# DeltaNet mixer with a top-2 MoE on one core: written-out steps, two load queues, and the FFN's residual sum moved from VectorE to TensorE and ScalarE

## The chip, the cores and the metric

One core of a Trainium2 chip runs the whole program. The metric is the device time of one execution in microseconds, median of several runs. TensorE is PE in the profile (PEld its weight loads), VectorE is DVE, ScalarE is ACT, GpSimd is POOL, SyncE is SP; SPq is the queue on which SyncE issues transfers.

## The reference

The input `x` is 8 x 192 x 16 x 16 in fp32: 8 sequences of 256 tokens with 192 channels. A mixer and an FFN follow each other, both with a residual sum.

```python
# mixer: t = layernorm over channels of x, heads of 16, 12 heads
q = l2norm(silu(t @ Wq)); k = l2norm(silu(t @ Wk)); v = silu(t @ Wv)
beta = sigmoid(t @ Wb)
# for every token, per head:
#   u_t = beta_t * (v_t - S_{t-1}^T k_t);  S_t = S_{t-1} + k_t u_t^T;  o_t = S_t^T q_t
x = x + (t + o @ Wo)
# FFN: h = layernorm(x), 8 experts of width 192, the top 2 weighted, a shared one of width 768
probs = softmax(h @ router_w); gates, idx = top_k(probs, 2), normalised
routed = sum_e dense_g[e] * ((silu(h @ w_gate[e]) * (h @ w_up[e])) @ w_down[e])
shared = (silu(h @ ws_gate) * (h @ ws_up)) @ ws_down
alpha = sigmoid(h @ sg_w + sg_b)
out = x + alpha * shared + (1 - alpha) * routed
```

## The kernel before

The 256 tokens are cut into 16 chunks of 16 tokens (`NC = 16`, `T = 16`); with 8 sequences a chunk has 128 tokens, one for each partition. A pipeline runs over steps c = -3 to 18. In step c, DVE runs the scan of chunk c, token by token. Around it the engines do the preparation of chunks c+1 to c+3 (functions `A_...`: norm, transposes, projections, silu, l2 norms), the mixer's output and the router of chunk c-1 (`Fa_...`, `G_...`), the FFN of chunks c-1 and c-2 (`Fb_...`, `unit`, `hidden`) and the result of chunk c-3 (`Fc_...`).

The scan on DVE has 16 iterations a step, and each iteration four operations, each done for two halves of the heads: `Pr` (L1150, product with the state), `u` (L1152, sum), `bank` (L1154, the key times u), `SH` (L1158, the new state). After each of these groups is a numbered slot, 64 a step, at which other DVE work is inserted by `at(slot, distance, function)`. The keys come from PE: `fill` (L358) multiplies `KR`, the keys of the chunk, with a selector, eight times a step for two iterations each; it waits until the state of an earlier pair is done. `KR` and `QB` (the queries, spread over partitions) are written to a scratch in DRAM and read back by SyncE's queue (`scratch_k`, `load_k`, `scratch_q`, `spread_q`). POOL multiplies states with queries (`reading`, `PQ` L778) and sums them up (`summing`, L785, L802). Its `rsqrt` (L767) makes the factors of both norms in one operation, for which DVE's `A_bias` waits.

The order of every engine's work in a step is a list written out by hand; semaphores alone couple the engines. Steps -3 to 3 and 12 to 18 are written out, steps 4 to 11 are a hardware loop of four turns with two steps each (`chunks`, L161 to L169). At the end of a step DVE waits for its chained operations and clears their semaphore `s_chain`; ACT and POOL clear theirs at the start of the next.

The FFN's hidden width is 12 units of 192 (`UN = 12`): 8 experts and 4 quarters of the shared one. Each unit is five fp32r matmuls of 384 columns (`Fb_up`, L397 to L401), because both operands are split into a high and a low part. ACT makes `sg` and `ug` from them (`unit`, L610, L611), POOL multiplies them (`hidden`, L823), PE transposes the product (`Fb_turn`, L409), ACT copies it (`hidden`, L621), and PE multiplies by `Wd` in fp32 (`Fb_down`, L421) in five groups into the bank `bDn`. DVE's `Fc_res` (L960) then adds the mixer's output `xh` to the bank, PE transposes `res` and ACT copies it into `xT`, which is stored.

The split of the up weights is made once, at the start. The first 128 rows come into `raw0`; ACT rounds them to `Whi0` (`weights_hi0`, L592) and POOL makes the rest (`weights_lo0`, L808). The last 64 rows come twice into the halves of `raw1`; ACT (`weights_hi1`, L601) and POOL (`weights_1`, L813) split them. All loads are issued by SyncE: in `load` before the first step `x` of four chunks, the projection weights, small weights and `raw0`; in `load_later` in step -1 the rest of `x`, `raw1` and `Wd`. In POOL's list of step 0, `weights_1(0)` and `weights_1(1)` stand ahead of `rsqrt(0)`.

Of the kernel before, what the change touches and what calls it, by code (L numbers as in the profile page):

```python
# [13 lines left out]
NC = L // T  # L14
P = 128
# [16 lines left out]
def build(nc, x, Wq, Wk, Wv, Wb, Wo, router_w, w_gate, w_up, w_down, ws_gate, ws_up, ws_down, sg_w, sg_b, out):  # L32
    ctx = ExitStack()
    with ctx:
# [128 lines left out]
        def chunks(eng, step):  # L163

            for c in range(-3, 4):
                step(c, c % 2)
            with eng.Fori(0, 4) as k:
                for j in range(2):
                    step(eng.snap(k * 2 + (4 + j)), j)  # L169
            for c in range(12, NC + 3):  # L170
                step(c, c % 2)

        def stage(c, par, d, fn, *args):

            n = c + d
            if not isinstance(n, int) or 0 <= n < NC:
                fn(n, (par + d) % 2, *args)

        def once(c, at, fn, *args):

            if isinstance(c, int) and c == at:
                fn(*args)

        def later(n, by):

            return not isinstance(n, int) or n >= by
# [9 lines left out]
        def scratch(slot, lo, n):  # L196

            return bKB[slot // 8 % 2][:, 2 * BR * G + lo:2 * BR * G + lo + n]

        @block.sync  # L200
        def _(sp):
# [41 lines left out]
            def load_up(i, to, lo, hi):  # L243

                for half, we, ws in ((0, w_gate, ws_gate), (H, w_up, ws_up)):
                    sp.dma_start(to[:, 0:E, half:half + H], we[:, lo:hi, :].rearrange("e c h -> c e h")).then_inc(s_wu[i], 16)  # L246
                    sp.dma_start(to[:, E:UN, half:half + H], ws[lo:hi, :].rearrange("c (s h) -> c s h", h=H)).then_inc(s_wu[i], 16)  # L247

# [5 lines left out]
            def load():  # L254
# [26 lines left out]
            def step(c, par):  # L281
# [5 lines left out]
                if isinstance(c, int) and c == -1:  # L287
                    load_later()
                if isinstance(c, int) and c == EARLY + 3:
                    sp.wait_ge(s_outc, EARLY)  # L290
                    store(0, EARLY * T)

            load()
            chunks(sp, step)
# [5 lines left out]
        def _(pe):  # L300
# [34 lines left out]
            def A_qk(a, p):  # L335
                if isinstance(a, int) and a == 0:
# [8 lines left out]
            def A_vb(a, p):  # L345
                if isinstance(a, int) and a == 0:
# [14 lines left out]
            def Fa_o(f, p):  # L361
                pe.wait_ge(s_otok, f + 1)
                pe.wait_ge(s_qks, f + 4 if not isinstance(f, int) else min(f + 4, NC))
                turn(bFa, otok).then_inc(s_ocp, 1)

            def Fa_y(f, p):
                if isinstance(f, int) and f == 0:
# [12 lines left out]
            def Fa_logits(f, p):  # L380
                if isinstance(f, int) and f == 0:
# [5 lines left out]
            def Fb_up(f, p, n):  # L387

                if isinstance(f, int) and f == 0 and n == 0:
# [23 lines left out]
            def Fb_down(f, p, g):  # L413
                lo, hi = GRP[g]
                if isinstance(f, int) and f == 0 and g == 0:
# [12 lines left out]
            def step(c, par):  # L428
                at = partial(stage, c, par)
                at(-2, Fb_up, 3)  # L430
                at(-3, Fb_down, 3)
                at(0, fill, 2)
                at(-2, Fb_up, 4)
                at(2, A_vb)
                at(2, A_qk)
                at(0, fill, 3)
                at(-2, Fb_up, 5)
                at(-1, Fa_o)
                at(-3, Fb_down, 4)
                at(0, fill, 4)  # L440
                at(3, A_x)
                at(-1, Fa_y)
                at(-2, Fb_turn, 0)
                at(-2, Fb_up, 6)
                at(-2, Fb_up, 7)
                at(-2, Fb_turn, 1)
                at(-2, Fb_up, 8)
                at(0, fill, 5)
                at(-3, Fc_out)
                at(-1, Fa_h)  # L450
                at(-2, Fb_up, 9)
                at(-2, Fb_up, 10)
                at(0, fill, 6)
                at(-1, Fa_logits)
                at(-2, Fb_turn, 2)
                at(-2, Fb_down, 0)
                at(0, fill, 7)
                at(-2, Fb_up, 11)
                at(-1, Fb_up, 0)
                at(-2, Fb_down, 1)  # L460
                at(1, fill, 0)
                at(-2, Fb_turn, 3)
                at(-2, Fb_down, 2)
                at(-1, Fb_up, 1)
# [3 lines left out]
                at(-2, Fb_turn, 4)  # L468

            pe.wait_ge(s_id, 2)  # L470
            pe.wait_ge(s_sel, T // 2)
            chunks(pe, step)

        @block.scalar
        def _(act):
# [9 lines left out]
            def A_xs(a, p):  # L485
                if later(a, 1):
                    act.wait_ge(s_xT, a)
                if isinstance(a, int) and a == FIRST:
# [90 lines left out]
            def Fa_exp(q, p):  # L579
# [3 lines left out]
                if isinstance(q, int) and q == 0:  # L583
# [38 lines left out]

            def Fc_out(q, p):
# [11 lines left out]
            def step(c, par):  # L635
                def table(n, name):

                    if (not isinstance(n, int) or 0 <= n < NC) and tables[0] != name:
# [3 lines left out]
                if n[0]:  # L642
                    act.sem_clear(s_act)
                    n[0] = 0
                at = partial(stage, c, par)
                at(-3, unit, 10)
                table(c - 2, LN_EXP)
                at(-2, Fa_exp)
                at(0, place, 0)
                table(c + 1, LN_EXP)  # L650
                at(1, A_inv)
                table(0, SILU)
                at(-3, hidden, 2)
                at(-3, unit, 11)
                once(c, 1, weights_hi1, 4)
                at(-2, unit, 0)
                at(2, A_h)
                at(2, A_xh)
                at(1, A_khi)
                once(c, 0, weights_hi0, 7)  # L660
                at(-3, hidden, 3)
                at(-2, unit, 1)
                once(c, 1, weights_hi1, 5)
# [543 lines left out]
```

## Time and profile before

| | us |
|---|---|
| median of 3 runs | 538.85 (537.14 to 539.02) |
| the profiled execution | 535.79 |
| its span, first to last instruction | 534.1 |
| mean granted TensorE clock | 0.938 of full |

The profile is of one execution. A timeline row gives start, length, engine, line, operation, written tile and read tiles, and in brackets how long the engine was idle before it and what released it. Rows with "x2" merge two operations of one kind. Matmuls overlap in time, so the distance of their starts says more than their lengths. "issue" in the chain is time in which the engine waited for nothing that the profile shows.

### The profile page before, as it was taken

The numbers are of one execution on the slowest core, as the hardware profiler recorded it, in microseconds if no ns is written. First come the engines' busy times: TensorE is split into PE (matmuls) and PEld (weight loads), VectorE is DVE, ScalarE is ACT, GpSimd is POOL, SyncE is SP. The second block draws the span as 40 slices with busy tenths as digits, with TensorE's granted clock in tenths as the row PEclk, the third lists the DMA queues.
The fourth block names the chain that finished last, engine by engine and source line by source line (L and its number), as shares of the span: only waits on it lengthen the run. The fifth ranks groups of instructions, "written<-read, shape, count | busy, mean of one in ns | idle before, by whom it ended". The sixth has DMA issues, their size and how long they took to land.

```text
span 534.1 us, 11599 instructions
## 1 busy us (share of the span) xinstructions
PE 439.0 (82%) x2464; PEld 384.2 (72%) x2464; DVE 435.6 (82%) x2546; ACT 330.8 (62%) x927; POOL 410.9 (77%) x525
## 2 busy tenths in 40 slices
PE   1552025799999999799979999899999998989996
PEld 0431013579888888688877978698988897979996
DVE  4177078999999999899979997999999999999300
ACT  2680053658585858485847767485858584746853
POOL 4471099989898989789895989698989899987341
PEclk9996555589999999999999999999999999999999
DMA  3659933232323222222222232313232323210300
GB/s 86 192 128 184 189 110 106 75 79 78 91 67 83 74 84 75 75 77 73 74 68 52 64 86 68 84 59 95 61 89 68 83 76 86 72 60 2 104 2 16
DMA packets 44682, 44.01 MB, mean 82 GB/s; under 512 B 19857, under 2 KB 36433, under 8 KB 44625
## 3 DMA queue, kind: packets, MB, share of 16 engines
q1 hardware_dynamic: 44624, 43.44, 31.2%
q14 instruction: 45, 0.36, 0.2%
q8 instruction: 13, 0.21, 0.2%
HBM read 37.13 MB, written 6.29 MB: 81 GB/s over the span
## 4 chain that ended last, share of the span: by engine, by line
DVE 65%; PE 10%; issue 6%; POOL 6%; SPq 6%; DMA 3%; ACT 1%; DVEq 1%; POOLq 0%; ACTq 0%
DVE Pr L1150 14%; DVE bank L1154 14%; DVE u L1152 14%; DVE SH L1158 12%; PE bank L421 3%; POOL PQ L778 3%; DMA W_unsplit<-in_L_ffn_ws_up_dram 2%; POOL PQ L785 2%; DVE st L907 2%; SPq L247 1%; DVE ss L991 1%; SPq L241 1%; PE bank L409 1%; SPq L246 1%; DVE mv L908 1%
## 5 line engine op out<-in xcount | busy, mean ns | idle before, releaser
L823 POOL TENSOR_TENSOR hid<-sg,ug 128x192 f32<-128x192 f32 x192 | 109.8, 598 | 39.4 <-ACT ug L611 36.9
L1150 DVE TENSOR_TENSOR Pr<-SH,bank 128x96 f32<-128x96 f32 x512 | 106.1, 251 | 17.8 <-ACT Pr L555 10.6
L778 POOL TENSOR_TENSOR PQ<-SH,QB 128x768 f32<-128x768 f32 x62 | 112.6, 1838 | 0.9 <-DVE SH L1158 0.9
L1154 DVE TENSOR_TENSOR bank<-bank,u 128x96 f32<-128x96 f32 x512 | 108.9, 261 | 0.0
L785 POOL TENSOR_TENSOR PQ<-PQ 128x768 f32<-128x768 f32 (+2 forms) x93 | 103.2, 1109 | 6.0
L1152 DVE TENSOR_REDUCE u<-Pr 128x6 f32<-128x102 f32 x512 | 107.7, 254 | 0.0
L421 PE MATMUL bank<-Wd,hidT 128*128 128x192 f32 x576 | 106.6, 326 | 0.0
L1158 DVE TENSOR_TENSOR SH<-SH,bank 128x96 f32<-128x96 f32 x512 | 106.2, 252 | 0.0
L421 PEld LDWEIGHTS bank<-Wd,hidT 128*128 128x128 f32 x576 | 93.7, 190 | 0.0
L610 ACT ACTIVATE sg<-bank 128x192 f32<-128x192 f32 x192 | 63.1, 329 | 44.1 <-PE bank L401 31.0
L358 PE MATMUL bank<-KR,Sel 128*128 128x384 f32 x128 | 55.1, 435 | 39.3 <-DMA KR<-k_scratch 25.6
L397 PE MATMUL bank<-Whi,hiT 128*128 128x384 f32 x192 | 73.9, 385 | 1.8 <-issue 1.8
L401 PE MATMUL bank<-W,loT 128*128 128x384 f32 x192 | 65.6, 342 | 0.0
L399 PE MATMUL bank<-Whi,loT 128*128 128x384 f32 x192 | 65.6, 341 | 0.0
L398 PE MATMUL bank<-Wlo,hiT 128*128 128x384 f32 x192 | 65.6, 341 | 0.0
L400 PE MATMUL bank<-W,hiT 128*128 128x384 f32 x192 | 65.4, 341 | 0.0
L358 PEld LDWEIGHTS bank<-KR,Sel 128*128 128x128 f32 x128 | 26.0, 205 | 44.5 <-DMA KR<-k_scratch 26.1
L611 ACT ACTIVATE ug<-bank,gate 128x192 f32<-128x192 f32 x128 | 53.4, 417 | 0.0
L621 ACT ACTIVATE hidT<-bank 128x512 f32<-128x512 f32 (+1 forms) x80 | 44.4, 555 | 14.3 <-PE bank L409 13.0
L639 ACT ACT_TABLE_LOAD x38 | 48.8, 1283 | 0.7
L409 PE MATMUL bank<-ident,hid 128*128 128x128 f32 x288 | 46.8, 280 | 0.4 <-POOL hid L823 0.2
L397 PEld LDWEIGHTS bank<-Whi,hiT 128*128 128x128 f32 x192 | 36.8, 192 | 5.0 <-issue 4.7
(146 smaller groups left out, 816.3 us busy)
## 6 DMA issues: line engine op xcount, KB each, us to landing
QB<-q_scratch SPq DMA_DIRECT2D x64, 384.0 KB
k_scratch<-khl SPq DMA_DIRECT2D x64, 48.0 KB, 2.6
KR<-k_scratch SPq DMA_DIRECT2D x32, 96.0 KB, 2.4
q_scratch<-qn SPq DMA_DIRECT2D x64, 24.0 KB, 1.6
Wd<-in_L_ffn_w_down_dram SPq DMA_DIRECT2D x1, 1152.0 KB, 12.7
out_dram<-xT SPq DMA_DIRECT2D x1, 896.0 KB, 4.1
Wlo_unsplit<-in_L_ffn_w_gate_dram SPq DMA_DIRECT2D x1, 768.0 KB, 5.4
Wlo_unsplit<-in_L_ffn_w_up_dram SPq DMA_DIRECT2D x1, 768.0 KB, 7.9
```

The lines of the kernel that those rows point to most:

```text
L358: mm(bKB[f % 2][:, 0:2 * BR * G], Sel[:, f].rearrange("p b x e -> p (b x e)"), KR[:, p, :], start=True, stop=True).then_inc(s_fill, 1)
L397: mm(to, hiT[:, p, 0:P], Whi0[:, n], start=True, stop=False)
L398: mm(to, hiT[:, p, 0:P], Wlo0[:, n], start=False, stop=False)
L399: mm(to, loT[:, p, 0:P], Whi0[:, n], start=False, stop=False)
L421: last = mm(bDn[:, 0:C], hidT[:, turn_half(g), k - lo, :], Wd[:, k, :], start=(k == 0), stop=(k == KT - 1))
L778: tt(PQ[:, at * BR * HP:(at + n) * BR * HP].rearrange("p (i b h) d -> p i b (h d)", i=n, b=BR), SH[:, lo:lo + n].rearrange("p i b h d -> p ...
L785: chained(tt(PQ[:, :, 0:w], PQ[:, :, 0:w], PQ[:, :, w:2 * w], ALU.add))
L823: tt(hid[:, r * H:(r + 1) * H], sg[:, m % RING], ug[:, m % RING], ALU.mult).then_inc(s_hid, 1)
L1150: v = each(lambda br: count(tt(Pr[:, br, i, :, 0:D], prev[:, br], KB[:, br], ALU.mult)), Sb)
L1152: v = each(lambda br: count(nc.vector.tensor_reduce(u[:, i % 2, br], Pr[:, br, i], X, ALU.add, negate=True)), v)
L1154: v = each(lambda br: count(tt(KB[:, br], KB[:, br], u[:, i % 2, br].unsqueeze(2).to_broadcast([P, HP, D]), ALU.mult)), v)
L1158: ins = tt(SH[:, i, br], prev[:, br], KB[:, br], ALU.add)
```

## The change

The hardware loop goes: all 22 steps are written out. The three clears of the chain semaphores go, and DVE's last wait of a step with them; the first iteration of a step waits for the state operations of the step before, half by half.

The first part of the up weights (`raw0`) is issued by ACT in step -3, after its first `A_xs`. The second part (`raw1`) moves into SyncE's `load`, before the first step. `load_later` keeps `x` and `Wd`.

DVE's `Fc_res` goes. PE puts one more product at the head of the down sum, identity times `xh`, into the same bank, and ACT copies the bank into `res`.

The lists of PE, ACT, POOL and DVE's slots are drawn anew. The step's border lies elsewhere in the lists: `Fb_up 3` and `4`, `fill 2`, `Fb_down 3`, `A_vb` and `A_qk` stand at the end of PE's list for the chunk that used to be handled at the start of the next step, and the same holds for ACT and POOL.

```diff
-        def chunks(eng, step):
-
-            for c in range(-3, 4):
+        def chunks(step):
+
+            for c in range(-3, NC + 3):
                 step(c, c % 2)
-            with eng.Fori(0, 4) as k:
-                for j in range(2):
-                    step(eng.snap(k * 2 + (4 + j)), j)
-            for c in range(12, NC + 3):
-                step(c, c % 2)
...
-                load_up(0, raw0, 0, C0)
+                load_up(sp, 1, raw1[0:C1], C0, C)
+                load_up(sp, 1, raw1[C1:P], C0, C)
 
             def load_later():
 
                 load_x(1, FIRST * T, L)
-                load_up(1, raw1[0:C1], C0, C)
-                load_up(1, raw1[C1:P], C0, C)
...
+                if g == 0:
+                    mm(bDn[:, 0:C], ident[:, :], xh[:, bass.ds(f, 1), :].rearrange("p z c -> p (z c)"), start=True, stop=False)
                 for k in range(lo, hi):
-                    last = mm(bDn[:, 0:C], hidT[:, turn_half(g), k - lo, :], Wd[:, k, :], start=(k == 0), stop=(k == KT - 1))
+                    last = mm(bDn[:, 0:C], hidT[:, turn_half(g), k - lo, :], Wd[:, k, :], start=False, stop=(k == KT - 1))
...
+            def Fc_res(q, p):
+                act.wait_ge(s_dg, q * NG + NG)
+                if later(q, 1):
+                    act.wait_ge(s_outp, q)
+                f(res[:, :], bDn[:, 0:C], ACT.Copy).then_inc(s_res, 1)
...
-            def Fc_res(q, p):
-                dve.wait_ge(s_dg, q * NG + NG)
-                if later(q, 1):
-                    dve.wait_ge(s_outp, q)
-                tt(res[:, :], bDn[:, 0:C], xh[:, bass.ds(q, 1), :].rearrange("p z c -> p (z c)"), ALU.add).then_inc(s_res, 1)
...
-                if n[0]:
-                    dve.wait_ge(s_chain, n[0])
-                if running:
-                    dve.wait_ge(s_pair, c * 8 + 8)
-                if n[0]:
-                    dve.sem_clear(s_chain)
-                n[0] = 0
```

The new lists, from the step's start (a stroke stands for the chunk after; only what the prediction speaks of is named in full):

```
PE    fill3 up5 down4 Fa_o A_x up6 Fa_y fill4 turn0 up7 up8 turn1 fill5 up9 Fc_out Fa_h fill6
      up10 up11 logits down0 turn2 fill7 down1 up0' turn3 fill0' up1' down2 fill1' up2' A_h
      turn4 up3' fill2' down3 up4' A_vb A_qk
ACT   A_xs (step -3: load raw0) place1 unit3 unit4 silu_v silu_qk Fa_oc sq unit5 unit6 hidden0
      unit7 Fc_res place0' Fa_h unit8 unit9 Fa_hT Fc_out unit10 hidden1 unit11 Fa_exp hidden2
      A_inv unit0' A_h A_xh A_khi hidden3 unit1' hidden4 A_hT unit2'
POOL  hidden6 rsqrt reading0 hidden7-10 summing0 hidden11 A_kn A_qn A_vn hidden0' reading1
      summing1 hidden1'-3' A_klo hidden4' hidden5'
DVE   slot 14 A_low, 19 A_z, 23 Fa_otok, 27 A_vT, 30 A_stats, 31 Fa_add A_var Fa_stats Fa_var,
      35 Fa_bias, 46 Fa_split, 47 A_ss A_bias, 48 to 58 router as before
```

Before, the same entries of PE read cyclically from `fill3`: `fill3 up5 Fa_o down4 fill4 A_x Fa_y turn0 up6 up7 turn1 up8 fill5 Fc_out Fa_h up9 up10 fill6 logits turn2 down0 fill7 up11 up0' down1 fill0' turn3 down2 up1' fill1' up2' A_h turn4 up3' down3 fill2' up4' A_vb A_qk`, and DVE had `A_z` at 20, `A_stats` at 31, `Fa_add Fa_stats A_var Fa_var` at 32, `Fa_bias Fc_res A_ss` at 36, `Fa_split` at 44, `A_vT` at 47, `A_bias` at 48. The splits of the up weights move too: `weights_1(0)` to `(3)` now stand at the end of POOL's list of step -1, behind `rsqrt(-1)`, and `weights_1(4)` to `(7)` in step 0 behind `rsqrt(0)`.

## Rows read from the trace of the kernel before

**Rows 1.** Page, parts 1 and 2: engines' busy time; clock and DMA by slices of 13.35 us.
```profile
PE 439.0 (82%) x2464; PEld 384.2 (72%) x2464; DVE 435.6 (82%) x2546; ACT 330.8 (62%) x927; POOL 410.9 (77%) x525
...
PEclk9996555589999999999999999999999999999999
...
DMA  3659933232323222222222232313232323210300
```

**Rows 2.** Page, part 4: the chain that ended last, by engine.
```profile
DVE 65%; PE 10%; issue 6%; POOL 6%; SPq 6%; DMA 3%; ACT 1%; DVEq 1%; POOLq 0%; ACTq 0%
```

**Rows 3.** Stretches, one step outside the loop: PE, PEld, DVE, ACT, POOL, clock, DMA.
```profile
131.50:158.30 26.80, 25.96 (x156) 23.21 (x155) 26.28 (x158) 19.18 (x57) 24.17 (x31) 1.00 0.30 79
```

**Rows 4.** Chain in order of time (start, us): first scan operations, a pause, last matmuls.
```profile
104.75 0.42 DVE Pr L1150 x2
...
131.31 0.42 DVE Pr L1150 x2
...
158.52 0.42 DVE Pr L1150 x2
...
212.77 2.80 issue
...
385.06 0.42 DVE Pr L1150 x2
...
411.88 0.42 DVE Pr L1150 x2
...
527.56 1.97 PE bank L421 x12
```

**Rows 5.** Chain in order of time, 210 to 217 us: what surrounds that pause.
```profile
212.71 0.06 DVEq L167
```

**Rows 6.** DVE timeline: start, length, line, operation, tiles, [idle before].
```profile
146.09 0.35 DVE L960 TENSOR_TENSOR res<-bank,xh 128x192 f32<-128x192 f32 x1
...
146.36 0.55 DVE L991 TENSOR_REDUCE ss<-sq 128x24 f32<-128x384 f32 x1
...
463.31 0.42 DVE L1150 TENSOR_TENSOR Pr<-SH,bank 128x96 f32<-128x96 f32 x2 [0.30 <-DVE SH L1158]
```

**Rows 7.** PE timeline, same step: a wait, and starts around a change of type.
```profile
140.21 0.33 PE L310 MATMUL bank<-ident,otok 128*128 128x128 f32 x1 [0.55 <-DVE otok L1021]
...
147.55 0.44 PE L397 MATMUL bank<-Whi,hiT 128*128 128x384 f32 x1
...
147.83 0.34 PE L398 MATMUL bank<-Wlo,hiT 128*128 128x384 f32 x1
...
148.01 0.34 PE L399 MATMUL bank<-Whi,loT 128*128 128x384 f32 x1
```

**Rows 8.** Timelines of SyncE's queue, DVE, ACT and PE, 0 to 80 us, in order of time.
```profile
15.13 2.45 SPq L247 DMA_DIRECT2D Wlo_unsplit<-in_L_ffn_ws_up_dram  x1
...
30.55 0.42 DVE L1150 TENSOR_TENSOR Pr<-SH,bank 128x96 f32<-128x96 f32 x2 [0.23 <-ACT Pr L555]
...
40.06 2.22 SPq L246 DMA_DIRECT2D W_unsplit<-in_L_ffn_w_gate_dram  x1
...
55.12 0.92 SPq L278 DMA_DIRECT2D Wd<-in_L_ffn_w_down_dram  x1
...
63.21 4.03 SPq L206 DMA_DIRECT2D k_scratch<-khl  x4
...
65.61 1.35 ACT L601 ACTIVATE hid<-W_unsplit 64x384 fp32r<-64x384 f32 x3 [24.06 <-DMA W_unsplit<-in_L_ffn_ws_up_dram]
...
68.85 0.15 DVE L925 TENSOR_SCALAR rstd<-rs 128x1 f32<-128x1 f32 x1 [18.44 <-POOL rs L767]
...
74.99 1.01 PE L358 MATMUL bank<-KR,Sel 128*128 128x384 f32 x2 [24.43 <-DMA KR<-k_scratch]
...
75.71 0.42 DVE L1150 TENSOR_TENSOR Pr<-SH,bank 128x96 f32<-128x96 f32 x2 [1.43 <-PE bank L358]
```

**Rows 9.** A stretch of 2 us in the start: columns as in rows 3.
```profile
18.00:20.00 2.00, 0.00 (x0) 0.00 (x0) 0.73 (x3) 1.92 (x5) 0.67 (x1) 1.00 1.08 332
```

More of the change, by code:

```diff
@@ L468, in step @@
                 at(-2, Fb_turn, 4)
+                at(-1, Fb_up, 3)
+                at(1, fill, 2)
+                at(-2, Fb_down, 3)
+                at(-1, Fb_up, 4)
+                at(3, A_vb)
+                at(3, A_qk)
             pe.wait_ge(s_id, 2)
             pe.wait_ge(s_sel, T // 2)
-            chunks(pe, step)
+            chunks(step)
         @block.scalar
@@ L648, in step @@
[L648 to L662, printed above, removed]
@@ L692, in step @@
                 once(c, 1, weights_hi1, 8)
+                once(c, 1, weights_hi1, 9)
+                at(1, place, 0)
                 at(-1, Fa_h)
-                at(-2, hidden, 1)
+                once(c, 1, weights_hi1, 10)
+                once(c, 1, weights_hi1, 11)
                 at(-2, unit, 8)
-                once(c, 0, weights_hi1, 1)
-                once(c, 1, weights_hi1, 9)
-                once(c, -1, weights_hi0, 6)
-                once(c, 0, weights_hi1, 2)
-                once(c, 1, weights_hi1, 10)
@@ L701, in step @@
-                once(c, 0, weights_hi1, 3)
+                at(-2, unit, 9)
                 at(-1, Fa_hT)
                 at(-3, Fc_out)
-                once(c, 1, weights_hi1, 11)
-                at(-2, unit, 9)
+                at(-2, unit, 10)
+                at(-2, hidden, 1)
+                at(-2, unit, 11)
+                once(c, -1, weights_hi0, 5)
+                table(c - 1, LN_EXP)
+                at(-1, Fa_exp)
+                at(-2, hidden, 2)
+                table(c + 2, LN_EXP)
@@ new lines, in step @@
+                at(2, A_inv)
+                table(0, SILU)
+                once(c, -1, weights_hi0, 6)
+                once(c, -1, weights_hi0, 7)
+                at(-1, unit, 0)
+                at(3, A_h)
+                once(c, 0, weights_hi1, 5)
+                at(3, A_xh)
+                at(2, A_khi)
+                once(c, -1, weights_hi0, 8)
+                at(-2, hidden, 3)
+                at(-1, unit, 1)
+                once(c, -1, weights_hi0, 9)
+                at(-2, hidden, 4)
@@ L773, in products @@
                     pool.wait_ge(s_QB[half], c * 32 + 32)
-                    if half or not isinstance(c, int) or c > 0:
+                    if half or c > 0:
                         pool.wait_ge(s_oT, c * 2 + half)
@@ L787, in reading @@
             def reading(c, p, half):
-                if half == 0 or not isinstance(c, int) or c < NC - 1:
+                if half == 0 or c < NC - 1:
                     products(c, half, 0)
@@ L792, in summing @@
             def summing(c, p, half):
-                if half == 1 and isinstance(c, int) and c == NC - 1:
+                if half == 1 and c == NC - 1:
                     return
```

240 lines of the change are left out of this document (114 added, 126 removed).

## Prediction, on record before the changed kernel ran

> **What bounds the kernel now.** I read five views, in this order: the page's totals, its chain, the chain in order of time, the timelines of single engines over one step, and the timelines of the first 80 us.
>
> The totals show no engine idle for long: PE and DVE are both busy for 82% of the span, POOL for 77% [rows 1]. The chain settles which of them counts: 65% of it is DVE, 10% PE, and 6% "issue", time in which nothing that the profile shows is awaited [rows 2]. So the kernel is three pieces: a start-up, the sixteen scan steps paced by DVE, and a tail after the scan.
>
> The scan can be measured by the starts of each step's first `Pr` operation. Step 2 starts at 104.75, step 3 at 131.31, step 4 at 158.52, step 12 at 385.06, step 13 at 411.88 [rows 4] and step 15 at 463.31 [rows 6]. Steps 4 to 11 are those of the hardware loop. Step 12, written out, takes 411.88 - 385.06 = 26.82 us; the eight loop steps take 226.54, or 28.32 each. The extra time has a visible part: a pause of 2.80 us on DVE at the back edge [rows 4], between two instructions of L167, the loop's own line [rows 5]. There are three such pauses in the chain.
>
> Within a written-out step DVE works almost without a gap (26.28 of 26.80 us). PE is busy for 25.96 of the same 26.80 [rows 3], so it is a near second: only 0.84 us of room, of which 0.55 is a wait for `otok` [rows 7]. POOL (24.17) and ACT (19.18) have more.
>
> The start-up holds one large stall. Step 0 starts at 30.55. Some thirteen of its sixteen iterations later DVE stops for 18.44 us, waiting for POOL's `rs`; POOL's list has `weights_1` ahead of it, which waits for ACT's `hid` L601, and that stood for 24.06 until the second half of the up weights had landed at 65.6. SyncE's queue was meanwhile still issuing loads (the second half's from 40.06 to 55.12, then `Wd`), and came to the keys of step 1 only at 63.21; PE's first matmul of step 1 ran at 74.99 and step 1 started at 75.71 [rows 8].
>
> **Part by part: steps written out.** The loop's eight steps at the length of step 12 take 8 x 26.82 = 214.56, so 11.98 less than now: 3 x 2.80 = 8.4 are the pauses, 3.6 the slower steps between them. Step 3, which ends with the entry to the loop, took 27.21 against 26.82: 0.4 more. Together -12.4 us. The instructions that run are the same ones, and a written-out step has no pause of that kind in the rows I read. (The Trainium skill, page Advanced Engine Details and Errata, section Control Flow Timing, gives a compare-and-branch about 108 ns. By it the three back edges would give 0.3 us back and the sum would be 8 us higher; the measured pause is 2.80 us each, and the row decides. The Trainium skill's page Runtime: NRT & Kernel Launch, section Instruction fetch mechanics, has a reason that no row here shows: a taken branch out of the fetched window must fetch its target.)
>
> **No clears.** Each step ends with DVE waiting for all its chained operations, then a semaphore clear. DVE stands idle for 0.30 us before the next step's first `Pr` [rows 6]. The wait for the state itself stays, but DVE can issue under it. I take the 0.30; over the 14 ends of steps 2 to 15, -4.2 us (bounds: nothing, if the state's own latency is the wait, and 4.2). The clears of ACT and POOL lie beside idle time and are costed at nothing.
>
> **The residual sum.** `Fc_res` leaves DVE: it starts at 146.09 and the next operation at 146.36 [rows 6], so 0.27 us. In steps 3 to 15, 13 x 0.27 = -3.5 us. It becomes one fp32 product of 192 columns on PE, which issues as two matmuls, ahead of the down groups. Twelve such take 1.97 us [rows 4], so two are 0.33 us. ACT gets a copy of about 0.33, hidden in its 7.6 us of room per step; if that cover were gone, 13 x 0.33 = 4.3 us. The copy waits for the last down group of the item before, and behind it stand `place(1, 0)`, `Fa_h` and `Fa_hT` in ACT's order; that group ran early in the step, so I expect no wait there. PE's `Fc_out` now stands behind `Up 9`, which covers the copy.
>
> **Orders redrawn.** Read cyclically, PE's, ACT's and POOL's lists are nearly the old ones: their start is turned by a few entries, and the operations keep their place against DVE's slots. What differs: `Fb_down 4` now stands ahead of `Fa_o`, so that it fills most of the 0.55 wait for `otok` [rows 7]; `logits` come one `Up` later and `Fa_split` two slots later; `A_vT` moves from slot 47 to 27, where its input was ready in the step before; `Fa_add`'s latency now hides `A_var` (at most 0.1 us a step, taken as nothing). Against it, PE changes from fp32 to fp32r 11 times a step instead of 9, and a first fp32r matmul after fp32 delays the next start to 0.28 instead of 0.18 [rows 7]: up to 0.2 us.
>
> This sets a new bound. DVE's step becomes 26.82 - 0.30 - 0.27 = 26.25. PE's need becomes 25.96 + 0.33 = 26.29 with no wait at all, and 27.13, if its 0.84 of waits stays as it is. The bounds of PE's excess over DVE are thus 0 (overlapping ends overstate its busy time) and 0.88 a step, 11.4 us over 13 steps. Since the largest wait is filled, I take the lower part: 0.1 a step, +1.3 us.
>
> **Up weights over two queues.** The first half (`raw0`, 2.3 MB by its shape) is issued by ACT, right after the first `xs`; the second half (another 2.3 MB, written twice into half the partitions) follows the small weights on SyncE at once, not after step 0's queries. What SyncE still has to load after these is `x` (1.15 MB) and `Wd` (1.7 MB).
>
> The cost: of the four issues of `raw0` the last alone held SyncE for 2.45 us [rows 8]. On ACT they stand ahead of `A_h(0)`, which all of chunk 0 follows; the projection weights, which DVE's split awaits, share the engines with `raw0`. And chunk 0's keys now queue behind the second half. I take 2.5 us of delay for step 0 (bounds 0, and 9: about 2 from the issues and 7 for 2.3 MB at the 332 GB/s of rows 9).
>
> The gain: the eight issues of the second half held SyncE's queue from 40.06 to 55.12 [rows 8], since it was full; the DMA engines were at 0.9 in these slices [rows 1]. With them gone from there, step 1's keys come 15.1 us earlier. Step 1 so starts at 75.71 - 15.1 + 2.5 = 63.1, an advance of 12.6. DVE would be there sooner: step 0 needs 19.9 us to its stall (68.85 - 18.44 - 30.55) and 5.4 from there to its end (75.71 - 1.43 - 68.85), 25.3 in all, so 30.55 + 2.5 + 25.3 = 58.4. The keys are what is late next. Step 1 took 104.75 - 75.71 = 29.04 with pauses that POOL's remaining weight work caused; step 2 took 26.56. I count 2.5 back. Start-up: -15.1 us (bounds -8.6 with all 9 of delay, -22.3 if step 1 waits for DVE alone and nothing is delayed).
>
> (A rule that speaks against this part is in the Trainium skill, page DMA: Bandwidth & Descriptors, section Issuing engines are not separate DMA queues: all issuers share the same 16 engines and a second one saves only issue time. By it two queues in themselves would give nothing and the sum would lose the whole 15.1 us; the stretch at 18 us shows the engines full, share 1.08, with one queue [rows 9], so the trace agrees. My gain rests on the order of the loads, not on their rate.)
>
> **Tail.** After the scan PE is full, and two residual products lie in it: +0.65 us.
>
> **Sum.** Span 534.1 - 12.4 - 4.2 - 3.5 + 1.3 - 15.1 + 0.65 = 500.9. The profiled execution took 535.79, 1.7 above its span: 502.6. The median of the runs, 538.85, lies 3 us above that execution, and their lowest, 537.14, 1.4 above; I forecast 503.5.
>
> **The rivals.**
> - TensorE becomes the pace: its 0.84 of waits stay beside the new product, 27.13 a step instead of 26.35, 13 x 0.78 = +10: 513.5. For it: 25.96 busy of 26.80. Against it: the largest wait is filled by the new order.
> - The loads hold the start anyway: the same bytes pass, now in front of step 0, and the 15.1 are not gained: 518.6. For it: engines at share 1.08 [rows 9]. Against it: over the first three slices they stood at 0.3, 0.6 and 0.5 [rows 1], so there is free time before 40 us for these bytes.
> - The start is hidden wholly: step 1 waits for DVE alone, and nothing is delayed, 7.2 us better: 496.3. Against it: 4.4 MB (`x`, `Wd` and the queries' 1.5) still pass ahead of step 1's keys.
> - Slower than before: PE's clock. It was granted at 0.5 (1.2 GHz) in the slices from 53 to 107 us [rows 1], while PE mostly waited for the scan's states and for keys. If it stays at 1.2 GHz in steps with full FFN work, PE's 26.3 us become up to 52.6, +26 a step. Two such steps more than now cancel the 35 us gained and give 503.5 + 52 = 555.5; it decides from 1.4 steps. For it: step 2 is now reached sooner. Against it: in the slice after PE had taken up its full work the clock was 0.8, by step 3 1.00 [rows 1, 3], and nothing in that changes.
>
> **How the numbers follow.** Forecast 0.62, TensorE 0.20, loads hold 0.07, start hidden 0.08, clock 0.02, and 0.01 that several small losses leave no change. Likeliest 503.5. The range reaches below the hidden start by 2 us of its bounds (494) and past the TensorE case (516); what it leaves out above is 0.10. About 0.5% (2.7 us) is what a measurement can tell from no change; faster 0.97, same 0.01, slower 0.02.
>
> **What would show it.** No pause of 2.8 us on DVE; steps 26.2 to 26.4 apart, with DVE's idle time before `Pr` at step ends gone. If TensorE is the pace, DVE's waits for `bank` L358 grow. In the start: ACT's `Whi` before 20 us, no 24 us wait of ACT or POOL, step 0 at 33, step 1 at 63.1 behind PE's wait for `KR`. Wrong would be: steps above 27, or step 1 after 70.

## The result and the profile after

The changed kernel takes 508.38 us (median of 4 runs, 507.11 to 509.27), the kernel before beside it 538.61 (4 runs): a ratio of 0.944, 95% interval 0.941 to 0.947. The forecast was 503.5 with a range of 494 to 516. The profiled execution took 509.27, with a span of 507.4; the prediction's sum for the span was 500.9, so 6.5 us are to be accounted for.

First the page of the changed kernel: busy times, granted clock and DMA share in slices of 12.7 us, and the chain by engine (they answer to [rows 1, 2]).

```profile
PE 438.0 (86%) x2496; PEld 391.9 (77%) x2496; DVE 431.1 (85%) x2530; ACT 330.8 (65%) x943; POOL 412.3 (81%) x525
...
PEclk9999999999999999999999999999999999999999
...
DMA  7939733232324232322323232323232323300300
...
DVE 64%; PE 14%; SPq 7%; POOL 6%; issue 3%; DMA 3%; ACT 1%; DVEq 0%; POOLq 0%; ACTq 0%
```

PE's and DVE's shares are up to 86% and 85%, in a span 26.7 us shorter. "issue" fell from 6% to 3% of the chain. In this execution PE's clock doesn't fall in the start: it is at 9 or more (the level of 2.4 GHz) in every slice. The DMA's load has moved to the front: slices 1, 2, 4 and 5 stand at 7, 9, 9 and 7.

One step, as [rows 3] (columns: length, then busy time of PE, PEld, DVE, ACT and POOL, clock, DMA share, GB/s):

```profile
120.90:147.30 26.40, 26.03 (x158) 23.87 (x157) 26.20 (x159) 19.29 (x58) 24.19 (x31) 1.00 0.29 80
```

Then the starts of steps 0, 1, 2, 3, 4 and 15, in DVE's timeline (start, length, engine, line, operation, tiles, in brackets the idle time before):

```profile
34.50 0.41 DVE L1143 TENSOR_TENSOR Pr<-SH,bank 128x96 f32<-128x96 f32 x2
...
67.37 0.42 DVE L1143 TENSOR_TENSOR Pr<-SH,bank 128x96 f32<-128x96 f32 x2 [7.41 <-PE bank L352]
...
94.56 0.42 DVE L1143 TENSOR_TENSOR Pr<-SH,bank 128x96 f32<-128x96 f32 x2
...
120.92 0.42 DVE L1143 TENSOR_TENSOR Pr<-SH,bank 128x96 f32<-128x96 f32 x2
...
147.27 0.42 DVE L1143 TENSOR_TENSOR Pr<-SH,bank 128x96 f32<-128x96 f32 x2
...
436.13 0.42 DVE L1143 TENSOR_TENSOR Pr<-SH,bank 128x96 f32<-128x96 f32 x2
```

No pause of 2.8 us [rows 4, 5] is left, nor the idle 0.30 ahead of `Pr` [rows 6]. A normal step takes 147.27 - 120.92 = 26.35 us, where 26.2 to 26.4 was forecast. From step 2 to step 15 it is 436.13 - 94.56 = 341.57 for thirteen steps, where the prediction had 340.3. From step 15's start to the end it is 71.3, forecast 70.87 (its own end without the 0.30 and without `Fc_res`, plus the residual products). So 1.3 + 0.4 of the 6.5 us arise after the start-up, and 4.9 in it: step 2 starts at 94.56, forecast 89.65. Step 1 starts at 67.37, forecast 63.1.

The start-up in timelines of ACT's queue, DVE, SyncE's queue and PE (beside [rows 8]):

```profile
6.96 2.30 ACTq L199 DMA_DIRECT2D Wlo_unsplit<-in_L_ffn_ws_up_dram  x1
...
15.04 0.47 DVE L965 CAST Wphi<-Wp 128x588 fp32r<-128x588 f32 x1 [6.30 <-DMA Wp<-in_L_conv_Wb_dram]
...
39.02 8.37 SPq L272 DMA_DIRECT2D Wd<-in_L_ffn_w_down_dram  x1
...
47.42 7.71 SPq L273 DMA_DIRECT2D Wd<-in_L_ffn_ws_down_dram  x1
...
55.18 3.69 SPq L207 DMA_DIRECT2D k_scratch<-khl  x4
...
66.65 1.01 PE L352 MATMUL bank<-KR,Sel 128*128 128x384 f32 x2 [12.08 <-DMA KR<-k_scratch]
```

ACT's last issue of `raw0` stood 2.30 us. One sign of the prediction failed here: ACT's `Whi`, expected before 20 us, is first written at 26.82. DVE's split of the projection weights came 4.5 us later than it does where `raw0` isn't loaded beside them (10.58, in experiment 6), and step 0 began at 34.50 instead of 30.55: 3.95 of delay, estimated 2.5. In the queue of SyncE the eight issues that had taken 15.1 us are gone, as said. But the two issues of `Wd`, which had taken 63.21 - 55.12 = 8.1 us [rows 8], now take 16.1, and the keys of step 1 begin at 55.18: only 8.0 earlier. (The second issue of `x`, just ahead of `Wd`'s, shrank from 5.38 us to 0.65.) PE waits 12.08 us for `KR`.

The same stretch as shares of time and rates, columns as above:

```profile
10.00:12.00 2.00, 1.31 (x4) 0.53 (x4) 0.00 (x0) 0.60 (x3) 0.00 (x0) 1.00 1.10 319
...
22.00:24.00 2.00, 0.00 (x0) 0.00 (x0) 1.09 (x5) 1.94 (x5) 0.69 (x1) 1.00 1.11 215
...
28.00:30.00 2.00, 0.98 (x5) 0.97 (x5) 0.42 (x1) 1.83 (x5) 1.97 (x3) 1.00 0.35 77
```

The 16 engines are full while the up weights pass (from 8 to about 27 us), and free at 28. The rate falls from 319 to 215 GB/s at the same share, when only `raw1`, whose transfers write 64 partitions each, is left.

### The profile page after: what moved, and what is told of

The parts are those of the page before. It is cut to its first block, busy times and chain, and to the rows that moved or that the text cites. A ratio compares the mean times of both kernels' runs of the same rounds, so it can differ in the third digit from the quotient of the medians.

```text
span 507.4 us, 10651 instructions
## 1 busy us (share of the span) xinstructions
PE 438.0 (86%) x2496; PEld 391.9 (77%) x2496; DVE 431.1 (85%) x2530; ACT 330.8 (65%) x943; POOL 412.3 (81%) x525
## 4 chain that ended last, share of the span: by engine, by line
DVE 64%; PE 14%; SPq 7%; POOL 6%; issue 3%; DMA 3%; ACT 1%; DVEq 0%; POOLq 0%; ACTq 0%
DVE Pr L1143 14%; DVE bank L1147 14%; DVE u L1145 13%; DVE SH L1151 11%; PE bank L417 5%; POOL PQ L779 2%; POOL PQ L786 2%; SPq L272 2%; DVE st L905 2%; SPq L273 2%; PE bank L403 1%; DMA k_scratch<-khl 1%; DMA Wp<-in_L_conv_Wb_dram 1%; PE bank L391 1%; PE bank L393 1%
## 5 line engine op out<-in xcount | busy, mean ns | idle before, releaser
L824 POOL TENSOR_TENSOR hid<-sg,ug 128x192 f32<-128x192 f32 x192 | 112.6, 602 | 39.6 <-ACT ug L607 19.1
L417 PEld LDWEIGHTS bank<-Wd,hidT 128*128 128x128 f32 x576 | 96.2, 190 | 0.0
L352 PE MATMUL bank<-KR,Sel 128*128 128x384 f32 x128 | 56.4, 445 | 22.5 <-DMA KR<-k_scratch 13.3
L403 PE MATMUL bank<-ident,hid 128*128 128x128 f32 x288 | 45.1, 275 | 0.0
L403 PEld LDWEIGHTS bank<-ident,hid 128*128 128x128 f32 x288 | 35.5, 141 | 4.0 <-issue 1.9
```

Of the source, the lines that this page charges most:

```text
L352: mm(bKB[f % 2][:, 0:2 * BR * G], Sel[:, f].rearrange("p b x e -> p (b x e)"), KR[:, p, :], start=True, stop=True).then_inc(s_fill, 1)
L403: last = tr(bHt[:, (k - lo) * P:(k - lo + 1) * P], hid[:, k % (KT // 2) * P:(k % (KT // 2) + 1) * P], ident[:, :])
L824: tt(hid[:, r * H:(r + 1) * H], sg[:, m % RING], ug[:, m % RING], ALU.mult).then_inc(s_hid, 1)
```

## The experiments

Ratios are to the kernel before on the same chip, with 95% intervals; each normal step is read between the starts of `Pr`. Spans are of the one traced execution, and among the four executions of one kernel they differ by up to 3.6 us (experiment 3). A difference of a few us is therefore read from where it arises in the trace: step 0, for one, starts at 34.3 to 34.8 in all seven traces with the changed kernel's order of loads ahead of it.

**1. Written out only.** The kernel before with its loop replaced, nothing else.

```diff
-            for c in range(-3, 4):
-                step(c, c % 2)
-            with eng.Fori(0, 4) as k:
...
+            for c in range(-3, NC + 3):
+                step(c, c % 2)
```

> The kernel before with the hardware loop written out and nothing else. Theory (the loop cost 12.4 us: three pauses of 2.8 and slower steps between them): steps 4 to 11 at 26.8 us each, span 521.7, ratio 0.977. Rival (the slower loop steps are not the loop's doing but the length of a full step): only the 8.4 us of the pauses go, steps 4 to 11 stay at 27.2, span 525.7, ratio 0.984. Rival (written-out code has to be fetched and stalls in its turn): no gain, ratio 1.00.

Measured: 524.59 us, ratio 0.974 (0.969 to 0.978), span 521.9. Two neighbouring steps in what used to be the loop, in DVE's timeline:

```profile
238.72 0.42 DVE L1145 TENSOR_TENSOR Pr<-SH,bank 128x96 f32<-128x96 f32 x2 [0.30 <-DVE SH L1153]
...
265.54 0.42 DVE L1145 TENSOR_TENSOR Pr<-SH,bank 128x96 f32<-128x96 f32 x2 [0.30 <-DVE SH L1153]
```

265.54 - 238.72 = 26.82, the length of step 12 before, and steps 4 to 12 take 26.81 to 26.85. The span fell by 12.2 us, forecast 12.4. The pause and the slow steps both belonged to the loop.

**2. No clears.** Experiment 1, and no clears or waits for them at a step's end; the first iteration waits for the state itself.

```diff
-                if n[0]:
-                    dve.wait_ge(s_chain, n[0])
-                if running:
-                    dve.wait_ge(s_pair, c * 8 + 8)
-                if n[0]:
-                    dve.sem_clear(s_chain)
-                n[0] = 0
```

> As the run with the loop written out, and without the waits and clears at the ends of steps. Theory: 0.3 to 0.4 us less a step, so steps at 26.5, span 4.2 to 5.6 us below that of the run with the loop written out. Rival (the next step's first product waits for the state anyway): no difference between the two.

Measured: 520.63 us, ratio 0.966 (0.962 to 0.970), span 518.6.

```profile
291.19 0.42 DVE L1141 TENSOR_TENSOR Pr<-SH,bank 128x96 f32<-128x96 f32 x2
...
317.68 0.42 DVE L1141 TENSOR_TENSOR Pr<-SH,bank 128x96 f32<-128x96 f32 x2
```

317.68 - 291.19 = 26.49, so 0.33 less a step, a little more than the 0.30 of idle time. From step 2 to step 15 that makes 4.0 us, since two of the thirteen steps took 26.67 and 26.84. Step 2 began at 105.47, 0.8 later than in experiment 1, for a reason that isn't known, so the span fell by 3.3 only, less than the 4.2 to 5.6 expected. The rival (no difference) is out.

**3. The loads only.** Experiment 1 with the new order of loads, all other orders old.

```diff
+                once(c, -3, load_up, act, 0, raw0, 0, C0)
...
-                load_up(0, raw0, 0, C0)
+                load_up(sp, 1, raw1[0:C1], C0, C)
+                load_up(sp, 1, raw1[C1:P], C0, C)
```

> The loop written out, and the up weights loaded as in the changed kernel (first half by ACT, second half ahead of step 0), with the old orders of work. Theory (the order of the loads makes the start-up gain): step 1 starts at about 67 as in the changed kernel instead of 75.7, span 8 to 11 us below the run with the loop written out. Rival (the gain needs the new places of the weight splits in POOL's and ACT's lists too): step 1 later than 70, or step 1 itself 29 us long as before instead of 27.2.

Measured: 512.79 us, ratio 0.950 (0.946 to 0.955), span 512.9. Starts of steps 0, 1 and 2:

```profile
34.77 0.42 DVE L1145 TENSOR_TENSOR Pr<-SH,bank 128x96 f32<-128x96 f32 x2 [0.22 <-PE bank L352]
...
67.78 0.42 DVE L1145 TENSOR_TENSOR Pr<-SH,bank 128x96 f32<-128x96 f32 x2 [7.80 <-PE bank L352]
...
94.60 0.42 DVE L1145 TENSOR_TENSOR Pr<-SH,bank 128x96 f32<-128x96 f32 x2 [0.30 <-DVE SH L1153]
```

Step 1 begins within 0.4 us of where the changed kernel has it, step 2 at the same time, 10.1 earlier than in experiment 1 (104.68). The order of loads alone makes the whole gain of the start-up. Of the 10.1, 1.1 are lost behind step 2, most of it in the last step, where DVE waits once for PE (0.82), so the span fell by 9.0. By the medians it is 11.8: the traced execution was the slowest of four here (spans 509.3 to 512.9) and the fastest of four in experiment 1.

**4. The sum back on DVE.** The changed kernel with `Fc_res` on DVE at slot 35, without PE's product and ACT's copy.

```diff
-                if g == 0:
-                    mm(bDn[:, 0:C], ident[:, :], xh[...], start=True, stop=False)
...
-                at(-3, Fc_res)
...
+                    at(35, -3, Fc_res)
```

> The changed kernel with the residual sum back on DVE (at slot 35) and neither the extra product nor ACT's copy. Theory (DVE paces the steps, PE's product lies in its idle time): steps of 26.36 become 26.63, span 3.5 us longer, the tail 0.65 shorter, ratio to the changed kernel 1.006. Rival (PE is as much the pace, so the move gave nothing): steps stay at 26.36 and the span is the same or shorter.

Measured: 509.6 us, ratio 0.944 (0.940 to 0.949), span 508.9.

```profile
307.53 0.42 DVE L1141 TENSOR_TENSOR Pr<-SH,bank 128x96 f32<-128x96 f32 x2
...
334.15 0.42 DVE L1141 TENSOR_TENSOR Pr<-SH,bank 128x96 f32<-128x96 f32 x2
```

334.15 - 307.53 = 26.62: the move is worth 0.26 us a step, estimated 0.27. The span differs from the changed kernel's by 1.5 only. From step 2 to step 15 the kernel takes 2.5 us more; 0.9 comes back at the end (step 15 and the tail take 70.4 here, 71.3 with the products on PE). The rest of 13 x 0.26 lies in step 2, which takes 26.36 in both kernels, and in one long step less (below). The expected 3.5 less 0.65 was missed by about half. The medians, 508.38 and 509.6, were taken on different chips, and the ratios to the kernel before are both 0.944. So the move's worth is shown in the steps; a net gain in time is not shown.

**5. `Wd` later.** The changed kernel, with the two issues of `Wd` behind SyncE's work of step 0, that is behind step 1's keys and queries.

```diff
                 if c == -1:
                     load_later()
+                if c == 0:
+                    load_down()
```

> The changed kernel with the load of Wd moved behind step 1's keys and queries. Theory (step 1 waits for its keys, which queue behind Wd on the same queue): PE's wait of 12.1 us for the keys and DVE's of 7.4 go, step 1 starts at about 60 instead of 67.4, span 7 us shorter, about 500. Rival (the keys are late for another reason, or Wd then delays step 2's): less than 3 us.

Measured: 501.87 us, ratio 0.932 (0.929 to 0.935), span 500.0. DVE's, PE's and SyncE's timelines:

```profile
34.38 0.41 DVE L1148 TENSOR_TENSOR Pr<-SH,bank 128x96 f32<-128x96 f32 x2
...
59.29 1.22 PE L357 MATMUL bank<-KR,Sel 128*128 128x384 f32 x2 [4.86 <-DMA KR<-k_scratch]
...
60.02 0.42 DVE L1148 TENSOR_TENSOR Pr<-SH,bank 128x96 f32<-128x96 f32 x2 [0.19 <-PE bank L357]
...
66.48 0.46 SPq L275 DMA_DIRECT2D Wd<-in_L_ffn_w_down_dram  x1
```

Step 1 starts at 60.02, and DVE was idle only 0.19 before it, though PE still waited 4.86 for `KR`: the keys now come just as DVE ends step 0. The span is 7.4 shorter, all of it at step 1 (67.37 - 60.02 = 7.35). `Wd` itself, issued at 66.48 with only the queries just ahead of it, takes 0.46 and 0.77 us of the queue instead of 8.37 and 7.71. The long issues have moved once more: the four of step 1's keys, now next behind the queries and `x`, take 8.4 us (42.43 to 50.87) instead of 3.69.

**6. `raw0` later.** The changed kernel, with ACT's four issues behind `A_hT(0)`.

```diff
-                once(c, -3, load_up, act, 0, raw0, 0, C0)
                 at(3, A_hT)
+                once(c, -3, load_up, act, 0, raw0, 0, C0)
```

> The changed kernel with ACT's four loads issued only after its copy of chunk 0's transposed input, about 11.9 us, instead of at 5.1. Theory (the first half of the up weights slows the projection weights on the shared DMA engines, by 4.4 us): the projection weights land near 10.7 as before the change, step 0 starts at 30.5 to 31.5 instead of 34.5; but step 1 waits for its keys behind Wd, so the span falls by less than 4, 0 to 4 us. Rival (the weights then come too late for the splits or for chunk 0's keys): step 0 not earlier, span the same or longer.

Measured: 511.24 us, ratio 0.949 (0.946 to 0.953), span 509.8.

```profile
10.58 0.47 DVE L965 CAST Wphi<-Wp 128x588 fp32r<-128x588 f32 x1 [2.06 <-DMA Wp<-in_L_conv_Wb_dram]
...
38.34 0.42 DVE L1143 TENSOR_TENSOR Pr<-SH,bank 128x96 f32<-128x96 f32 x2 [4.80 <-PE bank L352]
```

The projection weights are there at 10.58 again, but step 0 starts at 38.34, 3.8 later than in the changed kernel: the same bytes now keep the engines full until about 33 us, and the scratch round of chunk 0's keys stands in them. The expected start of step 0 (30.5 to 31.5) was missed, and the rival's account holds: what was saved ahead of the projection is paid at the keys.

**7. One queue.** The changed kernel, with both halves issued by SyncE, `raw0` first.

```diff
-                once(c, -3, load_up, act, 0, raw0, 0, C0)
...
+                load_up(sp, 0, raw0, 0, C0)
                 load_up(sp, 1, raw1[0:C1], C0, C)
```

> The changed kernel with both halves of the up weights issued by SyncE, first half first, none by ACT. Theory (one queue is served in order): the projection weights land near 10.7, but chunk 0's keys wait behind 4.6 MB, so step 0 starts at 35 to 38 and the span is 0 to 3 us longer than the changed kernel's. Rival (the second queue is what made the gain): step 0 after 40, span more than 5 us longer. Rival (the second queue was of no use): step 0 before 34.5, span shorter.

Measured: 513.41 us, ratio 0.953 (0.950 to 0.958), span 512.3, so 4.9 more than the changed kernel's. PE's first product of step 0's keys:

```profile
39.01 1.01 PE L353 MATMUL bank<-KR,Sel 128*128 128x384 f32 x2 [10.24 <-DMA KR<-k_scratch]
```

PE waits 10.24 us for chunk 0's keys, and step 0 starts at 39.73 instead of 34.50. The result lies between the first expectation and its rival. What it shows is that the second queue is worth about 5 us here, because its bytes start sooner: SyncE has 21 smaller issues ahead of `raw0` and comes to it at 13.30, ACT at 5.12. From 8 to 16 us the engines' share is 0.19, 0.33, 0.08 and 0.55 with one queue and 1.08 to 1.14 with two; the full stretch ends at about 34 us instead of 27.

**8. The product three times.** The changed kernel with the residual product made thrice (two surplus ones, 4 more issues on PE, 0.65 us a step).

```diff
-                    mm(bDn[:, 0:C], ident[:, :], xh[...], start=True, stop=False)
+                    for last in (True, True, False):
+                        mm(bDn[:, 0:C], ident[:, :], xh[...], start=True, stop=last)
```

> The changed kernel with the residual product made three times into the same bank (the first two are overwritten), 0.65 us more of PE work in each step. Theory (DVE is the pace and PE has about 0.4 us of room a step): steps grow by 0.25 us at most, from 26.36 to 26.6, the tail by 1.3; span 2 to 5 us longer. Rival (PE has no room left): 0.65 a step and in the tail, 10 us longer. Rival (PE has ample room): only the tail, 1.3 us.

Measured: 511.96 us, ratio 0.952 (0.949 to 0.955), span 509.3.

```profile
279.07 0.42 DVE L1144 TENSOR_TENSOR Pr<-SH,bank 128x96 f32<-128x96 f32 x2
...
305.49 0.42 DVE L1144 TENSOR_TENSOR Pr<-SH,bank 128x96 f32<-128x96 f32 x2
```

305.49 - 279.07 = 26.42: 0.65 us more of PE's work lengthens a step by 0.06. PE's room shows in its waits for DVE's `loT` (columns: us in all, times, longest), first in this kernel, 94 to 420 us:

```profile
PE bank L299 <- DVE loT L953: 0.5, 1, 0.5
```

and in the changed kernel, over the same stretch:

```profile
PE bank L299 <- DVE loT L952: 4.8, 12, 0.6
```

So 0.36 of the 0.65 us went into the waits for `loT`, 0.4 us a step; 0.06 lengthened the step, and where the other 0.2 went isn't traced. The changed kernel's PE is not the pace. With the surplus hardly a gap is left: it is busy in 288.69 of the 289 us from 121 to 410, against 284.66. The last step and the tail, where PE is busy throughout, took 1.9 us more (73.2 against 71.3).

**9. `A_bias` behind `Fa_max`.** Experiment 5, with DVE's `A_bias` (two operations, the factors `rstd` and `nmr`) moved from slot 47 to slot 48, between the router's maximum and its comparison.

```diff
-                    at(47, 3, A_bias)
                     at(48, -1, Fa_max)
+                    at(48, 3, A_bias)
```

> The kernel with Wd behind step 1's keys, and DVE's A_bias moved back from slot 47 to slot 48, between the router's maximum and the table of differences that waits for it. Theory (the new slots cost DVE 0.13 us a step, as the difference between 26.62 with the sum on DVE in the new slots and 26.49 in the old ones shows, because A_bias no longer covers the maximum's latency): steps of 26.35 become 26.2 to 26.25, span 1.5 to 2 us shorter. Rival (the 0.13 comes from another slot): steps stay at 26.35.

Measured: 500.17 us, ratio 0.927 (0.922 to 0.932), span 498.1, the best kernel of the study. First the stretch of DVE's timeline in the changed kernel:

```profile
378.46 0.15 DVE L923 TENSOR_SCALAR rstd<-rs 128x1 f32<-128x1 f32 x1
...
378.64 0.21 DVE L925 TENSOR_SCALAR nmr<-mv,rs 128x1 f32<-128x1 f32 x1
...
378.78 0.41 DVE L1143 TENSOR_TENSOR Pr<-SH,bank 128x96 f32<-128x96 f32 x2
...
379.18 0.15 DVE L1020 TENSOR_REDUCE negmax<-bank 128x1 f32<-128x8 f32 x1
...
379.37 0.23 DVE L1028 TENSOR_TENSOR bank<-bank,logit 128x64 f32<-128x64 f32 x1
```

`nmr` starts 0.18 behind `rstd`, and the comparison (L1028, `bank`) 0.19 behind `negmax`, which it needs; `logit` and `negmax`, which don't depend on each other, start 0.08 apart. Together `rstd` to `Pr` and `negmax` to the comparison take 0.32 + 0.19 = 0.51. The same in experiment 9:

```profile
369.29 0.41 DVE L1148 TENSOR_TENSOR Pr<-SH,bank 128x96 f32<-128x96 f32 x2
...
369.69 0.15 DVE L1025 TENSOR_REDUCE negmax<-bank 128x1 f32<-128x8 f32 x1
...
369.77 0.14 DVE L928 TENSOR_SCALAR rstd<-rs 128x1 f32<-128x1 f32 x1
...
369.94 0.21 DVE L930 TENSOR_SCALAR nmr<-mv,rs 128x1 f32<-128x1 f32 x1
...
370.07 0.22 DVE L1033 TENSOR_TENSOR bank<-bank,logit 128x64 f32<-128x64 f32 x1
```

`rstd` and `nmr` now lie inside the wait for `negmax`: from `negmax` to the comparison it is 0.38 for all of it, 0.13 less. And the starts of two steps:

```profile
297.25 0.42 DVE L1148 TENSOR_TENSOR Pr<-SH,bank 128x96 f32<-128x96 f32 x2
...
323.46 0.64 DVE L1148 TENSOR_TENSOR Pr<-SH,bank 128x96 f32<-128x96 f32 x2
```

323.46 - 297.25 = 26.21, 0.15 less than in the changed kernel. Between the medians of experiments 5 and 9 that is 1.7 us.

**10. All the old slots.** Experiment 9, with DVE's other slots put back to where they were before (`A_z` 20, `A_stats` 31, `Fa_add` and `A_var` at 32, `Fa_bias` and `A_ss` 36, `Fa_split` 44), except `A_vT`.

```diff
-                    at(47, 2, A_ss)
+                    at(36, 2, A_ss)
...
-                    at(46, -1, Fa_split)
+                    at(44, -1, Fa_split)
```

> The kernel with Wd behind step 1's keys, and all of DVE's slots as before the change, except A_vT, which stays at 27. Theory (the new slots cost 0.13 us a step somewhere): steps of 26.35 become 26.22, span 1.7 us shorter. Rival (the lists of the other engines need the new slots): waits of PE for otok or loT or of ACT for norms grow, and steps are 26.35 or longer.

Measured: 501.59 us, ratio 0.930 (0.925 to 0.935), span 499.9; steps uneven, 26.25 to 26.75, where 26.22 was expected. From step 2 to step 15 it takes 2.3 us more than experiment 9, and the rival, that the other engines' lists need the new slots, has the better of it. The engine that is late is POOL (timelines of POOL and DVE, step 4):

```profile
148.46 0.36 POOL L808 TENSOR_TENSOR oT<-PQ 128x96 f32<-128x96 f32 x1
...
148.85 0.38 DVE L1020 STREAM_TRANSPOSE otok<-oT 128x192 f32<-128x192 f32 x1
```

`otok` starts 0.03 behind the end of POOL's `oT`, and 0.34 behind the operation of DVE ahead of it, instead of 0.16; in experiment 9 `oT` is done 0.3 before. In step 7, where `otok` is 0.03 late only, the step takes 26.25. So little is lost by the old slots on DVE itself; what they lose is POOL's lead.

**11. `raw1` behind step 0's queries.** Experiment 10 with `raw0` in SyncE's `load`, `raw1` at the head of `load_later`, and nothing on ACT's queue.

```diff
-                load_up(sp, 1, raw1[0:C1], C0, C)
-                load_up(sp, 1, raw1[C1:P], C0, C)
+                load_up(sp, 0, raw0, 0, C0)
...
             def load_later():
+                load_up(sp, 1, raw1[0:C1], C0, C)
+                load_up(sp, 1, raw1[C1:P], C0, C)
                 load_x(1, FIRST * T, L)
```

> As the kernel with the old slots, and the first half of the up weights issued by SyncE at the end of load, the second half behind step 0's queries, ahead of the rest of x; none by ACT. Theory (the DMA engines are full from 7 to 27 us, and whoever comes first delays the others): step 0 starts at 30.5 as before the change, step 1 waits for keys behind the second half and x until about 61 or for DVE until 56; span the same as with the old slots, plus or minus 3. Rival (the second half comes too late for POOL's splits ahead of rsqrt): DVE waits for rs in step 0 for 3 us or more, and the span grows by 2 to 8.

Measured: 518.16 us, ratio 0.960 (0.955 to 0.965), span 516.1. ACT's and DVE's timelines:

```profile
61.62 0.93 ACT L603 ACTIVATE hid<-W_unsplit 64x384 fp32r<-64x384 f32 x2 [23.78 <-DMA W_unsplit<-in_L_ffn_ws_up_dram]
...
64.74 0.37 DVE L910 BATCH_NORM_STATS2 st<-bank 128x6 f32<-128x192 f32 x1 [20.77 <-PE bank L319]
```

The span is 16.1 us longer than experiment 10's, where the rival expected 2 to 8. Step 0 started at 30.49, as before. But `raw1` had landed only at 61.6, ACT waited 23.78 us for it, what ACT owed PE came late, DVE stood for 20.77, and step 1 began at 76.89. This is the old stall of [rows 8] under other names, now with `Wd` out of the way. It isn't the queue of `raw0`: in experiment 7 SyncE issued that too, with `raw1` right behind it, and step 1 began at 72.44 without such a stall. So the early place of `raw1` is what removes it, and the late place of `Wd` is worth the further 7.4 (experiment 5).

## Why the prediction was right, and where it was off

**Steps written out: right.** -12.2 us of span in experiment 1, forecast -12.4. A taken back edge cost DVE what the row said (2.80 us). The Trainium skill's page Advanced Engine Details and Errata, section Control Flow Timing, gives about 108 ns for a compare-and-branch; that figure can't be used for DVE's back edge of this loop.

**No clears: right.** 0.33 us a step in experiment 2, forecast 0.30; 4.0 us from step 2 to step 15 and 3.3 of the span, forecast 4.2.

**The residual sum: right.** 0.26 us a step on DVE in experiment 4, forecast 0.27; ACT's copy cost nothing to be seen. Its price in the tail came out at 0.9 us by experiment 4, forecast 0.65, and over the span the move gave 1.5 net, forecast 2.9. By the traced spans the four gains, 12.2 (experiment 1), 3.3 (2), 9.0 (3) and 1.5 (4), make 26.0 of the 26.7 us by which the span fell.

**PE's excess, "0.1 a step, +1.3 us": right in size, wrong in cause.** The step lasts 26.36 instead of 26.25. The prediction charged the 0.1 to PE. Experiment 8 loaded PE with 0.65 more and got 0.06; PE had room. As forecast, the wait for `otok` was filled (2 waits of PE from 94 to 420 us, against 12 in experiment 2). Experiment 9 gave 0.15 back by moving one function of DVE. The prediction went through the redrawn slots of DVE without a price for `A_bias` at 47 instead of 48; the loss was there. The sum closes without PE: 26.49 (experiment 2) less 0.26 or 0.27 is 26.22 to 26.23, and experiment 9 shows 26.21. Steps 2 to 14 took 1.3 us more than the whole forecast for them; 0.9 of that are the two long steps below.

**The start-up, "-15.1 us": the step that was mis-sized.** It measured -10.2 (step 2 at 94.56 instead of 104.75), with 4.3 us of the miss at step 1 and 0.6 in step 1's length (27.19). Two terms were off.

"With them gone from there, step 1's keys come 15.1 us earlier" took the time that SyncE spent in its issues as their own cost. It is the time in which the queue drains what is ahead: with the eight issues gone, `Wd`'s two behind them took over 8.1 us of it (16.1 for 8.1), because `x`, the queries and `Wd` were still to pass. Against that, the issues of the queries and of `x` ahead of `Wd` took 5.4 us less (35.07 to 39.02, before 30.74 to 40.06 with 5.38 in one issue of `x`). So the queue term was worth 12.4 us and not 15.1. Experiment 5 shows it from the other side: with `Wd` behind the keys its issues cost 1.2 us together. The rival "the start is hidden wholly" had named these bytes as the reason against it; the sum should have had the same reason in it.

The delay was estimated at 2.5 us, of bounds 0 and 9. It was 3.95 at the start of step 0 and 4.3 where SyncE's queue issues step 0's queries; it is the engines' share taken from the projection weights. The two terms, 2.7 and 1.8, less 0.3 by which the way from the keys' first issue to step 1 was shorter (12.2 against 12.5), are the miss at step 1 to 0.1. Experiments 6 and 7 moved the bytes of `raw0` later in two other ways, and step 0 came later in both (38.34 and 39.73). The prediction also gave the second queue no worth of its own; experiment 7 puts it at 4.9 us.

**The rivals.** TensorE as the pace (513.5): against it, experiment 8. Loads that hold the start (518.6): experiment 3 gained 9.0 us by the loads alone. A start hidden wholly (496.3): not in this kernel; experiment 5 comes near it, with step 1 at 60.0. The clock: the page of the profile shows 9 in every slice, and among the four runs the one with a mean granted clock of 0.93 took 507.11 and one with 1.00 took 509.27, so it did not set the time.

**Not settled.** One or two steps of each of the kernels without clears are 0.2 to 0.5 us longer than their neighbours, at places that go with the kernel (here and in experiments 5 to 9 steps 5 and 11: 26.72 and 26.89 here, 0.9 us in all; in experiment 2 steps 5 and 8, in experiment 4 step 8 alone). At the end of step 5 the chain has 0.40 of "issue" ahead of `Pr`. In step 11 DVE starts `Pr` 0.43 after `nmr`, where the same two starts lie 0.14 apart in experiment 9's first rows (378.64 and 378.78):

```profile
351.97 0.21 DVE L925 TENSOR_SCALAR nmr<-mv,rs 128x1 f32<-128x1 f32 x1
...
352.40 0.42 DVE L1143 TENSOR_TENSOR Pr<-SH,bank 128x96 f32<-128x96 f32 x2 [0.21 <-issue]
```

With the clears such a step doesn't stand out (experiments 1 and 3, steps 4 to 11, 26.81 to 26.85). No run tells what it is.

## What to carry to other kernels

When a queue's issues are long, as SyncE's were here, they measure what is queued ahead of them and not their own cost: take away some, and the next ones take over the time, unless the bytes are gone too. Ask which transfer is late at which consumer, and put what is needed last (`Wd`) behind it; this one move was worth 7.4 us. In a step paced by one engine's chain, look for operations that stand right behind the one that they need: one of them shifted by one place gave 0.15 us a step, half as much as an operation taken off the engine. Where an engine off the chain has only 0.3 us of lead, as POOL has ahead of `otok`, a slot moved on the pacing engine can use it up (experiment 10).

## What the hardware showed that was not expected

The back edge of the loop held DVE for 2.80 us (2.85 and 2.76 at the next two), and no other engine so long. At the first turn, from the branch to the next instruction of the loop's own line, DVE took 2.86 us (212.71 to 215.57), ACT 0.28 (203.35 to 203.63), POOL 0.30, SyncE 0.32 and PE 0.40. What sets DVE apart isn't shown.

The loads of `raw1`, which write 64 partitions each, moved 191 to 222 GB/s with the 16 engines full (16 to 26 us); those that write 128 moved 319 to 332 ([rows 9] and above). `raw1` also reads its rows a second time, and no run separates the two.

The Trainium skill's page DMA: Bandwidth & Descriptors, section Issuing engines are not separate DMA queues, says that transfers started by different engines run on the same 16 DMA engines. The trace agrees: the share didn't rise with the second queue (1.10 against 1.08). What the second queue changed is when the bytes started (experiment 7).

An issue of the same `Wd` load stood for 8.37 us in a queue with bytes ahead and for 0.46 us with only the queries just ahead (experiment 5).
